# Node numbers and attention weights held in PSUM, and a feed-forward stage joined with its layer norm, in a four-network graph kernel

## The reference, cut to what matters

```python
# L0: graph attention, 4 heads, 3 rounds
att = ln(gat(x) @ w_ao.T + b_ao + x, ln1_g, ln1_b)
inter = gelu(att @ w_int.T + b_int)              # 128 -> 512
m = ln(inter @ w_out.T + b_out + att, ln2_g, ln2_b)   # 512 -> 128
h = gru(m, h);  x = ln(h, ln3_g, ln3_b)
# L1: agg = segment_sum(x[src], dst); two linear layers, batch norm
# L2: 4 rounds: a = segment_sum(trans[etypes, src], dst); h = gru(a, h)
# L3: transformer attention, 8 heads
s = exp(clip(sum(K[src] * Q[dst] / 4, axis=-1), -5, 5))
wV = segment_sum(V[src] * s, dst);  z = segment_sum(s, dst)
h_attn = wV / (z + 1e-6)                          # then linear, norm, ffn, norm
```

## Time and profile before

| what | value |
|---|---|
| median of 3 runs | 9637.24 us (9629.43 to 9647.61) |
| profiled execution | 9634.97 us, of which the span of the trace is 9633.1 us |
| PE busy in the span | 6180.4 us (64%) |
| POOL busy | 6121.9 us (64%) |
| DVE busy | 4480.6 us (47%) |
| ACT busy | 1958.9 us (20%) |
| mean granted TensorE clock | 0.779 |

### The profile page before, as it was taken

How to read it: one execution, slowest core, us unless ns; L and a number is a source line. 1 busy time by engine, 2 the same in 40 slices (tenths; PEclk the granted TensorE clock), 3 DMA queues, 4 the chain that set the end, 5 groups by cost and what they waited for, 6 DMA issues and landing times. The chain is left out here.

```text
span 9633.1 us, 134269 instructions
## 1 busy us (share of the span) xinstructions
PE 6180.4 (64%) x31445; PEld 4879.4 (51%) x31446; DVE 4480.6 (47%) x9847; ACT 1958.9 (20%) x3826; POOL 6121.9 (64%) x6482
## 2 busy tenths in 40 slices
PE   4888777887777886774445446444644644476666
PEld 3666655666646665643443444344444434445554
DVE  5555745555845556742223223222422322257775
ACT  2444134444044443140001000000100000021112
POOL 2777425776417775517774777677677767747773
PEclk7999889999889998985556557655855765588887
DMA  3555523555604554502222222222222222233332
GB/s 88 159 159 159 162 63 101 159 159 148 189 3 144 159 159 126 164 23 52 52 52 78 52 52 77 61 52 52 86 52 52 78 61 52 52 98 103 103 103 64
DMA packets 708449, 916.18 MB, mean 95 GB/s; under 512 B 148175, under 2 KB 448091, under 8 KB 708078
## 3 DMA queue, kind: packets, MB, share of 16 engines
q0 software_dynamic: 198368, 429.61, 17.5%
q1 hardware_dynamic: 487108, 441.09, 14.6%
q10 hardware_dynamic: 22730, 42.81, 1.2%
HBM read 702.69 MB, written 210.24 MB: 95 GB/s over the span
## 5 line engine op out<-in xcount | busy, mean ns | idle before, releaser
L1016 POOL DMA_INDIRECT states<-table_typed,tile_idx x2512 | 2436.6, 970 | 992.4 <-issue 785.1
L999 POOL DMA_INDIRECT states<-table_x,src_idx x2016 | 1907.0, 946 | 721.5 <-issue 592.3
L1103 PE MATMUL psum<-states,select 128*128 x4480 | 1006.0, 401 | 1142.2 <-DVE t L1089 1060.8
L1103 PEld LDWEIGHTS psum<-states,select 128*128 128x128 f32 x4480 | 894.7, 298 | 1276.2 <-issue 1275.8
L1066 DVE SCALAR_TENSOR_TENSOR select<-dst_all,pair_start,iota_row 128x512 f32<-128x512 f32 x560 | 420.6, 751 | 1765.4 <-SPq L1113 1573.0
L1500 PE MATMUL psum<-wt,l_scores_mixT 128*128 128x256 f32 x4032 | 996.5, 390 | 39.3 <-issue 34.2
L1103 PE MATMUL psum<-states,l_update_select 128*128 x2688 | 578.4, 389 | 547.7 <-DVE t L1089 547.7
L1507 PE MATMUL psum<-t,l_scores_spread 128*128 x4032 | 586.7, 289 | 426.6 <-DVE score L1465 415.2
L999 POOL DMA_INDIRECT l_pass_ring<-table_kv,src_idx x672 | 659.7, 982 | 298.7 <-issue 196.1
L1103 PEld LDWEIGHTS psum<-states,l_update_select 128*128 128x128 f32 x2688 | 516.6, 288 | 622.8 <-issue 622.8
L1500 PEld LDWEIGHTS psum<-wt,l_scores_mixT 128*128 128x128 f32 x4032 | 730.1, 191 | 200.1 <-issue 109.3
(11 more groups left out here) (407 smaller groups left out, 9479.9 us busy)
## 6 DMA issues: line engine op xcount, KB each, us to landing
rows_dram<-l_scores_values SPq DMA_DIRECT2D x504, 264.0 KB
t<-rows_dram SPq DMA_DIRECT2D x504, 264.0 KB, 3.0
states<-in_edge_attr_dram SPq DMA_DIRECT2D x2016, 64.0 KB
states<-table_typed,tile_idx POOLq DMA_INDIRECT x2512
table_typed<-states ACTq DMA_DIRECT2D x36, 1024.0 KB, 4.4
states<-table_x,src_idx POOLq DMA_INDIRECT x2016
table_x<-select SPq DMA_DIRECT2D x50, 256.0 KB, 2.3
l_pass_ring<-table_kv,src_idx POOLq DMA_INDIRECT x672
```

The costliest lines, as they stand in the source:

```text
L999: pool.indirect_dma_start(out=ring[:, k % REGIONS, u, :], out_offset=None, in_=table, in_offset=at).then_inc(gathered[k % REGIONS], 16)
L1016: pool.indirect_dma_start(out=ring[:, k % TILE_RING, u, :], out_offset=None, in_=table, in_offset=at).then_inc(gathered[k % REGIONS], 16)
L1103: ins = pe.matmul(psum[:, k % 2, 0:P], picked(more, k)[:, u, :], slots[:, bass.ds(at[u], D)], start=u == 0, stop=u == GROUP - 1)
```

## The change

Three parts. In the walks the compare takes the node numbers from PSUM bank 7, where ScalarE copies them at the start of each pass (`node_no`); in the last three turns of an update pass, where bank 7 serves other results, it keeps `iota_row`. In the transformer pass ScalarE writes the exponential twice, to a PSUM bank (`weights`), from which VectorE weighs the values, and behind the message as before; TensorE waits for this second write with a semaphore of its own. The feed-forward of L0 and the norm behind it become one block, `transformed`, in which each turn handles chunk t in the feed-forward and chunks t-1 to t-3 in the norm. It has its own set of norm semaphores.

```diff
-        n_added, n_turned, n_measured, n_varied, n_rooted, n_inverse, n_scaled, n_rows, n_back, n_kept, n_eps = sems(
-            "state_added", "nodes_turned", "nodes_measured", "nodes_varied", "nodes_rooted", "nodes_inverse", "nodes_scaled", "nodes_normed",
-            "turned_back", "norm_kept", "norm_eps")
+        Norm = namedtuple("Norm", "turned measured varied rooted inverse scaled rows back kept eps")
+        norms = [Norm(*sems(*(f"nodes_{step}{k}" for step in Norm._fields))) for k in range(2)]
+        n_turned, n_measured, n_varied, n_rooted, n_inverse, n_scaled, n_rows, n_back, n_kept, n_eps = norms[0]
+        n_added, = sems("state_added")
...
+        def turn_nodes(pe, src, c, added=False, first=0, depth=IN, n=norms[0]):
...
-        def layer_norm(name, src, dst, eps, gain, shift):
...
         p_iota, = sems("node_numbers_in_bank")
+        node_no = psum[:, BANKS_USED, 0:P]
...
-        def pick(dve, more, s, k, column, needs):
+        def pick(dve, more, s, k, column, needs, numbers):
...
-                scalar=pair_start[:, bass.ds(s, 1)], in1=iota_row[:].unsqueeze(1).broadcast_to([P, GROUP, P]),
+                scalar=pair_start[:, bass.ds(s, 1)], in1=numbers.unsqueeze(1).broadcast_to([P, GROUP, P]),
                 op0=ALU.subtract, op1=ALU.is_equal).then_inc(p_selected, 1)
 
         def first_picks(dve, more):
 
+            dve.wait_ge(p_iota, 1)
             entries = by_step(dve, walk_row, 0, 3 * LEAD, NP)
             for s in range(LEAD):
-                pick(dve, more, s, s, entries[3 * s], entries[3 * s + 1])
+                pick(dve, more, s, s, entries[3 * s], entries[3 * s + 1], node_no)
...
-        def pick_and_add(dve, more, i, after=None):
+        def pick_and_add(dve, more, i, after=None, numbers=node_no):
...
-                    pick(dve, more, s + LEAD, k + LEAD, column, needs)
+                    pick(dve, more, s + LEAD, k + LEAD, column, needs, numbers)
...
-                            pick_and_add(dve, more, i, after)
+                            pick_and_add(dve, more, i, after, iota_row[:])
...
+                        act.copy(node_no, iota_row[:]).then_inc(p_iota, 1)
                         for c in range(CHUNKS):
...
+                weights = psum[:, 3, 0:GROUP * L3_HEADS].rearrange("p (u h) -> p u h", h=L3_HEADS)
...
-                                act.activation(msg[:, r % 2, :, D:W], part[:, r % 2, :, :], ACT.Exp, scale=HD ** -0.5).then_inc(p_weight, 1)
+                                act.activation(weights, part[:, r % 2, :, :], ACT.Exp, scale=HD ** -0.5).then_inc(p_weight, 1)
+                                act.activation(msg[:, r % 2, :, D:W], part[:, r % 2, :, :], ACT.Exp, scale=HD ** -0.5).then_inc(p_placed, 1)
...
-                                                  msg[:, r % 2, :, D:W].unsqueeze(3).broadcast_to([P, GROUP, L3_HEADS, HD]),
+                                                  weights.unsqueeze(3).broadcast_to([P, GROUP, L3_HEADS, HD]),
...
+                                pe.wait_ge(p_placed, region_of(i, r) + 1)
                                 pe.wait_ge(p_weighted, region_of(i, r) + 1)
...
+        def transformed(name, state, sums, function, w_in, b_in, w_out, b_out, eps, gain, shift):
+
+            K, SUM, FIRST, DEPTH = len(w_in), 4, 5, 2
+            n = norms[1]
+            with ExitStack() as tmp:
+                inner = sb(f"{name}_inner", [P, V, K, CHUNK], F32, tmp)
+                rows = select[:, 0:V, :, :]
+                with block(name, d_turned, d_mixed, d_product, d_done, *n) as b:
+                    @b.tensor
+                    def _(pe):
+                        def expand(c):
+                            for k in range(K):
+                                at_least(pe, d_mixed, (c - 1) * K + (k + 1))
+                                pe.matmul(psum[:, k, :], w_in[k], state[:, at(c)], start=True, stop=True).then_inc(d_turned, 1)
+
+                        def contract(c):
+                            at_least(pe, d_done, c)
+                            for k in range(K):
+                                pe.wait_ge(d_mixed, c * K + (k + 1))
+                                ins = pe.matmul(psum[:, SUM, :], w_out[k], inner[:, c % V, k, :], start=k == 0, stop=k == K - 1)
+                            ins.then_inc(d_product, 1)
+                        for t in range(CHUNKS + 3):
+                            if t < CHUNKS:
+                                expand(t)
+                            if 1 <= t <= CHUNKS:
+                                pe.wait_ge(d_done, t)
+                                turn_nodes(pe, sums, t - 1, first=FIRST, depth=DEPTH, n=n)
+                            if t >= 3:
+                                turn_back(pe, rows, t - 3, 1, FIRST, DEPTH, n)
+                            if t < CHUNKS:
+                                contract(t)
+
+                    @b.scalar
+                    def _(act):
+                        def bend(c):
+                            at_least(act, d_product, c - (V - 1))
+                            for k in range(K):
+                                act.wait_ge(d_turned, c * K + (k + 1))
+                                act.activation(inner[:, c % V, k, :], psum[:, k, :], function, bias=b_in[k]).then_inc(d_mixed, 1)
+                        act.wait_ge(n.eps, 1)
+                        for t in range(CHUNKS + 3):
+                            if t < CHUNKS:
+                                bend(t)
+                            if 2 <= t < CHUNKS + 2:
+                                normalise(act, rows, t - 2, ACT.Identity, FIRST, DEPTH, n)
+                            if t >= 3:
+                                keep_norm(act, state, t - 3, 1, gain, shift, first=FIRST, depth=DEPTH, n=n)
+                            if 1 <= t <= CHUNKS:
+                                root(act, t - 1, n)
+
+                    @b.vector
+                    def _(dve):
+                        def finish(c):
+                            dve.wait_ge(d_product, c + 1)
+                            dve.scalar_tensor_tensor(out=sums[:, at(c)], in0=psum[:, SUM, :], scalar=b_out, in1=state[:, at(c)],
+                                                     op0=ALU.add, op1=ALU.add).then_inc(d_done, 1)
+                        dve.memset(eps_t[:], eps).then_inc(n.eps, 1)
+                        for t in range(CHUNKS + 2):
+                            if t >= 2:
+                                scale(dve, t - 2, n)
+                            if 1 <= t <= CHUNKS:
+                                measure(dve, t - 1, FIRST, DEPTH, n)
+                            if t < CHUNKS:
+                                finish(t)
...
-            feed_forward("l0_ffn", xT, t1, ACT.Gelu, parts_of(wt, WINT, GAT_FF), [wcol("b_int", k) for k in range(GAT_FF)],
-                         parts_of(wt, WOUT, GAT_FF), wcol("b_out"))
-            layer_norm("l0_ln2", t1, xT, 1e-12, wcol("ln2_g"), wcol("ln2_b"))
+            transformed("l0_ffn", xT, t1, ACT.Gelu, parts_of(wt, WINT, GAT_FF), [wcol("b_int", k) for k in range(GAT_FF)],
+                        parts_of(wt, WOUT, GAT_FF), wcol("b_out"), 1e-12, wcol("ln2_g"), wcol("ln2_b"))
```

More of the change, by code:

```diff
@@ L12 @@
 from contextlib import ExitStack, contextmanager
+from collections import namedtuple
 from itertools import count
@@ L751, in normalise, with root @@
+        def root(act, c, n=norms[0]):
+            act.wait_ge(n.varied, c + 1)
+            act.activation(std[:, of4(c)], moment[:, of4(c), 1], ACT.Sqrt, bias=eps_t[:], scale=1.0).then_inc(n.rooted, 1)
+        def normalise(act, rows, c, function, first=0, depth=IN, n=norms[0]):
+            act.wait_ge(n.scaled, c + 1)
+            at_least(act, n.back, c - (V - 1))
             for k in range(4):
-                ins = act.activation(rows[:, c % V, k, :], psum[:, first + c % IN, k * P:(k + 1) * P], function,
+                ins = act.activation(rows[:, c % V, k, :], psum[:, first + c % depth, k * P:(k + 1) * P], function,
@@ L760, in keep_norm @@
                 if gain is None:
[L761 removed]
+                    ins = act.copy(to[:, at(c)], psum[:, first + depth + c % banks, :])
                 else:
[L763 to L797 removed]
@@ L799, in node_rows @@
+                    ins = act.activation(to[:, at(c)], psum[:, first + depth + c % banks, :], ACT.Identity, bias=shift, scale=gain)
+            ins.then_inc(n.kept, 1)
         def node_rows(name, src, dst, eps, gain=None, shift=None, gain_rows=None, also=None, plus=None, queries=False):
```

91 lines of the change are left out of this document (26 added, 65 removed).

## The result

The changed kernel takes 9508.2 us, the median of four runs (9507.7 to 9523.0). The kernel before took 9636.4 beside it (9629.4 to 9647.6). The ratio is 0.987, with a 95% interval of 0.9858 to 0.9883: 128 us faster. Forecast were 92 us and a range that began at 9515. The time lies 7 us outside it.

A forecast was written before the change was run, and what follows sets the result against it. POOL's gathers were taken to bound the walks and transformer pass, PE the L0 feed-forward. Gains of 55 + 13 + 24 = 92 us from 9634.97 gave 9543 us; range 9515 to 9590.

The forecast's parts named there:

- part 3: Joined feed-forward and norm stage, three rounds: TensorE sets the pace, gain 24 us, bounds -40 and +33.
- the fill: Start of the joined stage: 3.0 us of slower start, as in the kernel before.
- the end: Tail of the joined stage: finish 0.95, last transposes 1.1, statistics to kept state 7.15, handover 0.3 us.
- Part 1: Walks: one SBUF input of each looped selection goes, so gathers shorten; gain 55 us, bounds 0 and about 65.
- The signs: Mixing pass: POOL busy about 593 us instead of 607; looped steps: no gather over 1.0 us beside a selection.
- Part 2: Transformer pass: weights in PSUM stop the weighing from lengthening gathers; gain 13 us, bounds 0 and 20.
- rival 3: Transformer pass: the short selections L1021 take over the weighing's stalls, no gain there; 9556 us, chance 8%.
- 1 (POOL not relieved): Gather stages: long gathers come from any long VectorE instruction or what it writes; 9611 us, chance 4%.
- 2: Joined stage: ScalarE becomes the bound through its table loads, a turn 10.5 us; 9600 us, chance 7%.
- 4: Joined stage: PE and ACT take turns instead of overlapping, a turn 16.5 us; 9780 us, chance 4%.
- The 65 ns: Walks: by the skill, each of 824 changed selections 65 ns longer, 54 us of VectorE time, covered by slack.

The follow-up runs named there:

- e10: e5's kernel with each of the joined stage's first four transposes issued twice; 11451.8 us, the kernel before 11446.3.
- e13: e6's kernel with added products into an unused bank in each chunk of the old norm; 9654.4 us, 7.0 more than e6.
- e9: e6's kernel with only the joined feed-forward and norm stage added; 9596.0 us, -51.4 against e6.
- e7: e6's kernel with only the walks' looped selections reading node numbers from PSUM; 9593.1 us, -54.3 against e6.
- e5: The changed kernel with max(number, 0) ahead of each engine wait on a table number; 9524.9 us against 9640.1 for the kernel before.
- e8: e6's kernel with only the transformer's weights put in PSUM; 9628.2 us, -19.2 against e6.
- e15: e5's kernel with each PSUM selection's operation done once more into a spare place, node numbers in PSUM; 9520.5 us, ratio 0.9873 to the kernel before.
- e14: e5's kernel with each PSUM selection's operation done once more into a spare place, node numbers in SBUF; 9699.7 us, ratio 1.0063 to the kernel before.
- e11: e5's kernel with Relu in place of Gelu in the joined stage, so no table changes there; 11438.5 us, the kernel before 11446.3.
- e6: The kernel before with max(number, 0) ahead of each engine wait on a table number; 9647.4 us against 9635.4 without it.
- e16: e5's kernel with the update passes' last selections, gate and new state also in PSUM; 9757.8 us, the kernel before 9642.4.
- e1: The changed kernel with four tables of awaited numbers as 16-bit instead of 32-bit integers; 11902.6 us, the kernel before 11441.8.
- e18: e5's kernel once more, on a chip where the kernel before took 11444.0 us; 11445.1 us.

## Why the prediction was wrong, point by point

**The failed step** is in part 3: "four transposes take 0.86 (1414.28 to 1415.14)", and with it "a full turn: 2 x 3.43 + 2 x 0.86 = 8.58 us". It took the products' price from a block with the clock at 0.96 and the transposes' from one at 0.63 (0.50 in the very stretch), and put both into a stage in which TensorE has no gap. There the clock is 1.00 and four transposes take 0.43: a turn of 7.74. Sixteen groups at 0.43 too much are 6.9 us a round, 21 of the 27 us that part 3 was off; e10 (0.44 us for four more in the dense stage) and e13 (0.44 instead of 0.85 in the old norm, once its clock is at 1.00) show both halves of it. The rest is the fill, 1.8 to 2.9 us instead of 3.0, and the end, 8.3 us from the last product to the kept state instead of 9.5. Part 3 gave 51 us (e9), above its stated upper bound of 33, since that bound varied the end and held the transposes' price fixed. That is why the range missed, too.

**Part 1** was right in mechanism, place and size: 55 us forecast, 54.3 measured (e7); mixing pass 14.3 forecast, 14.2 measured. The signs came as named: POOL busy 594.0 us, no gather of the mixing pass above 983 ns. In e5 the update passes keep 4.4 to 6.6 us over 628 x 0.944 each, where some 6 were left in. The reason given was too wide in one point: that the operation is running just after the start isn't enough, it must have begun before the gather, by 0.08 us or more.

**Part 2** was right in mechanism, too small in size: 13 forecast, 19.2 measured (e8), 18.0 in the gathers' busy time (659.6 to 641.6). The forecast let go what stood under L1688 and kept the 5.5 us it gave to L1021. Most of that went as well: the gathers whose first 0.35 us met one of L1021's selections were 5.9 us over 944 ns each before (235 gathers, 30 of them over 970 ns), and 1.2 us in e8 (282, 12 over 970). The phases did shift, as rival 3 had it, but to the better. Why to the better wasn't tried. The one gather of 5.4 us over stays.

**Rivals.** 1 (POOL not relieved) is refuted by e15 beside e14. The inference in the Trainium skill, "SBUF — State Buffer", section "Who interferes with whom", that a two-input operation leaves the descriptor generation of GpSimd's DMAs alone, didn't help here: an operation with two SBUF tensors lengthened 165 of 174 gathers in e14. The forecast left out what the same section states beside it, that a VectorE instruction with two SBUF inputs contends with a GpSimd instruction that reads SBUF. A gather reads its indices there (`tile_idx`), so e14 and e15 agree with that; which access of the gather it is that waits, no run shows. 2 and 4 are refuted by the turn of 7.74 us and by e11; 3 by e8. The loads took 1.283 us each and what followed them began 0.01 us later; the drain of 1380 ns that the Trainium skill adds to each ("ScalarE: Activation LUTs", section "What ACT_TABLE_LOAD costs") would not fit into a turn of 7.74 us with two loads and 4.8 us of other work in it. ScalarE waits for only 0.35 us of a turn, half of the 0.7 that the forecast left it: it would be the next bound of this stage. The forecast's 54 more loads were 48. The 65 ns for a source in PSUM, worked out from the Trainium skill's "VectorE: DVE Perf Modes", section on the TRN2 errata, weren't seen either: the selection's mean went from 751 ns to 747.

**The sum.** 124.9 measured apart against 92: walks -1, transformer +6, stage +27. The execution's own gathers (3 ns, 17 us) account for the step from 9508 to 9523, the bounded numbers (12 us in e6) and e5's chip (4 us) for that from 9508 to 9525.

## What to carry to other kernels

A row has the clock of its stretch. Before a duration is carried into a stage that will be dense, look at the granted clock where it was read and take a row of the same instruction at the level that the new stage will have; vary this price in the range. While GpSimd issues gathers one by one, look for VectorE operations with two tensors in SBUF that begin shortly before a gather's start and still run after it: here 0.74 us more of VectorE work a step cost nothing with one tensor in PSUM, and 179 us in all with both in SBUF. But a value kept in a bank makes the bank's next writer wait; e16 lost 231 us in all, with 23 us less of gathering.

## What the runs showed of the hardware that was not expected

- The same operation, 824 times, costs 179 us with its second tensor in SBUF and nothing that can be told with it in PSUM (e14, e15), by lengthening gathers on another engine by 254 ns on average.
- The order of the starts decides, too: the gathers that such a selection begins 0.10 to 0.55 us ahead of are all long, and those that it begins at most 0.07 us ahead of, or behind, are not (153 of 153 and 0 of 111 before). Just ahead of a gather the selection itself is longer, 779 ns on average against 750 (33 selections begun about 0.05 us ahead).
- Transposes of 128x128 (L712) come 0.11 us apart at a granted clock of 1.00 and 0.21 at 0.50 (e13, e6).
- Loads of numbers into registers: 20 16-bit numbers took TensorE 4.7 us (e1), 20 32-bit numbers 1.4 (e18). VectorE's 140 loads of 21 32-bit numbers in the walks of e5 start at 12 x (7k + 3) bytes of the table: 35 took 1.6 us, as many as start at a multiple of 16 (in the mixing pass it is these seven), and the other 105 took 4.7 or more.
- Chips differ: the kernel before takes 9640 us on some and 11440 on others, with POOL busy for 6075 us (e1) as for 6058 in the profile after, and on the second kind the change was worth nothing that can be told (e18 beside before: 0.9998, 0.9987 to 1.001).
